# Last self-attention of a two-layer perceiver block: weighed V with columns in rows, exponentials divided before the weighing, the weighing one step later

## Chip, cores, metric

One core of one Trainium2 chip. The metric is the device time of one execution in microseconds (us), the median of several runs. Engines: PE or TensorE (matmuls, transpositions through an identity), VectorE (DVE), ScalarE (ACT), GpSimd (POOL), and SyncE (SP), which issues DMAs.

## The reference, cut to what matters

Six sublayers act on x of 128 batches x 32 tokens x 256 features: cross-attention, self-attention, a mixture of experts, cross-attention, self-attention (the one changed), and a linear layer with quantised weights and activations. The last two:

```python
qkv = einsum('bse,ef->bsf', layernorm(x), W_qkv)      # 256 -> 3 x 16 heads x 64
q, k = rotary(q), rotary(k)
scores = einsum('bqhd,bkhd->bhqk', q, k) / sqrt(64)    # 32 x 32 for each batch and head
weights = softmax(where(mask, scores, -1e9))           # causal mask
out = einsum('bhqk,bkhd->bqhd', weights, v)            # batch, 32, 16 x 64
x = x + einsum('bsf,fe->bse', out, W_out)              # 1024 -> 256
...
x = x + bit_linear(layernorm(x), weight)               # rounded to whole numbers, 256 -> 256
```

## The kernel before, in words

The kernel is written for the engines directly: each engine has a queue of its own in program order, and semaphores hold it where it needs another's result. Each sublayer is a stage. The last stage, `SelfAttention1`, does the last self-attention and the quantised linear layer (`BitLinear`).

The 4096 rows of x are 32 groups of 128 rows (4 batches of 32 tokens, `BPG` = 4). The stage is a loop of 42 steps g, written out by hand in `steps()`: in step g every engine does its share of group g (projections, rotation), of group g-1 (scores and softmax), of group g-2 (attention turned, projected out and added to X), of group g-3 (statistics for the last norm), and of the linear layer of group g-9 (`last`). Once in four steps come the jobs for four groups together: with g mod 4 = 1 the norm's statistics (`ln.take_stats`), with 2 its scaling, with 3 its transposition on PE (`ln.turn`, 8 transposes) and its split into a high and a low part on ScalarE and VectorE (`prepare`); and, from step 6 on, `quantise` with g mod 4 = 3 and `round_z` with g mod 4 = 0, on VectorE.

For float32 precision the projections are split products: every 128-row piece of weights and data is taken as high and low part in three matmuls, so one projection `project(g, i, c)` (i = 0, 1, 2 for Q, K, V, c the half of 512 columns) is 6 matmuls of 512 columns, and `project_out` is 24 of 256 columns. All these stand under line L223. Plain float32 matmuls (scores L865, weighing L914) are two instructions each in the trace.

PE's order in a step: project (0,0), (0,1); `turn_out(g-2, 0)` (4 transposes of the attention output, L1870); project (1,0), (1,1); `turn_out(g-2, 1)`; `turn` (0,0), (0,1) (rotated Q, L1857); scores(g-1) (64 products, 128 instructions); project (2,0); turn (1,0); `project_out(g-2)`; `ln.turn` in every fourth step; turn (1,1); project (2,1); `bit.turn` (2 transposes into bank z, L1750); weigh(g-1) (64 products, L914); `bit.product` (2 bfloat16 matmuls, L1767).

VectorE's order: rotate (0,0), (0,1); `attn_lo` 0; rotate (1,0), (1,1); `attn_lo` 1; softmax(g-1); the projected attention of g-2 added to X (L2031, which empties bank o); prepare; the norm's statistics or scaling; the last norm's statistics of g-3; quantise or round_z; the attention of g-1 divided by the sums out of PSUM (L2052); `bit.add` (L1774). ScalarE's: `attn_hi` 0, 1; `keep_turned` (0,0), (0,1); the exponentials of g-1 (L871); `keep_v` 0 (L1937); `keep_turned` (1,0); prepare; `keep_turned` (1,1); `keep_v` 1; `bit.keep_turned` (zT for the product, L1758). GpSimd adds the two halves of each rotation (L2067). The data all lie in SBUF here; the only DMAs are the loads of weights before the loop and eight stores of the result.

PSUM has 8 banks: two for the scores, two for the weighed V, and four in a `Ring` that hands them out in turn: a `take` gets the next of the four, and PE waits until the tile taken four takes before has been emptied by its reader (`s_v` for V, `r_swap` for Q and K, `r_qkT` for rotated tiles, `xT_lo` for the norm, `s_x1` for bank o, `bit_zT` for z, `bit_x` for the linear layer's product).

Of the kernel before, what the change touches and what calls it, by code (L numbers as in the profile page):

```python
# [16 lines left out]
P = 128  # L17
# [93 lines left out]
class Signals:  # L111


    def __init__(self, nc, stack):
# [14 lines left out]
        for tag, names in (("x0", "qkvo"), ("s0", "qkv"), ("moe", ("router",)), ("x1", "qo"),  # L129
# [31 lines left out]
        self.s_score, self.s_max, self.s_shift, self.s_exp, self.s_probT, self.s_inv, self.s_pv, self.s_out = (  # L161
            count("s_" + n, grid(SELF, g)) for n in ("score", "max", "shift", "exp", "probT", "inv", "pv", "out"))
        self.s_sum = count("s_sum", grid(("s1",), g))
# [23 lines left out]
        self.a_T, self.a_hi, self.a_lo = (count("a_" + n, grid(g, half)) for n in ("T", "hi", "lo"))  # L187
# [646 lines left out]
class HeadOrder:  # L834


    def __init__(self, R, head, cells):
        self.R, self.NH = R, H // R
        self.cells = cells
        self.column = {head(r, n): (r * self.NH + n) * T for r in range(R) for n in range(self.NH)}  # L840


class SelfSoftmax:


    def __init__(self, s, tag, order, tiles, score, scale, bound):
        self.s, self.tag, self.order, self.t, self.score, self.scale, self.bound = s, tag, order, tiles, score, scale, bound

    def cell(self, a):
        return a.rearrange("p (r n q) -> p r n q", r=self.order.R, q=T)  # L850

    def stat(self, a):
        return a.rearrange("p (r n) -> p r n", r=self.order.R)

    def scores(self, pe, g, q_k):
        s, tag, R = self.s, self.tag, self.order.R
        if g:
            if self.bound is None:
                pe.wait_ge(s.s_shift, tag, g - 1)
            else:  # L860
                pe.wait_ge(s.s_masked, g - 1)
        for heads, q, k in q_k(g):
            for b in range(BPG):
                for r in range(R):
                    ins = pe.do.matmul(self.score[b * T:(b + 1) * T, r, heads, :], q(b, r), k(b, r), start=True, stop=True)  # L865
        ins.then_inc(*s.s_score.at(tag, g))

    def exponent(self, act, g):
        s, tag, e = self.s, self.tag, g % 2
        act.wait_ge(s.s_shift, tag, g)  # L870
        act.do.activation(self.t["prob"][e][:, :], self.t["shifted"][e][:, :], ACT.Exp,  # L871
                          scale=self.scale if self.bound is None else 1.0).then_inc(*s.s_exp.at(tag, g))

    def softmax(self, dve, g):
        s, tag, t, e = self.s, self.tag, self.t, g % 2
        R, NH = self.order.R, self.order.NH
        src = self.score
        dve.wait_ge(s.s_score, tag, g)
        if g >= 2:
            dve.wait_ge(s.s_exp, tag, g - 2)  # L880
            dve.wait_ge(s.s_probT, tag, g - 2)
            dve.wait_ge(s.s_out, tag, g - 2)
        if self.bound is not None:
            for r in range(R):
                ins = dve.do.scalar_tensor_tensor(out=self.cell(t["shifted"][e][:, :])[:, r], in0=self.score[:, r], scalar=self.scale,
                                                  in1=self.bound.unsqueeze(1).to_broadcast([P, NH, T]), op0=ALU.mult, op1=ALU.min)
            ins.then_inc(*s.s_masked.at(g))
            dve.wait_ge(s.s_masked, g)
            src = self.cell(t["shifted"][e][:, :])
# [6 lines left out]
        if g >= 2:  # L896
            dve.wait_ge(s.s_pv, tag, g - 2)
# [5 lines left out]
        if len(own.shape) == 4:  # L903
            sums = sums.rearrange("p r (m e) -> p r m e", m=own.shape[2])
# [1329 lines left out]
```

## Time and profile before

| what | value |
|---|---|
| median of 3 runs | 2792.21 us (2787.71 to 2792.39) |
| profiled execution, time | 2789.23 us |
| profiled execution, span of its instructions | 2787.4 us |
| PE busy | 2515.0 us, 90% |
| VectorE busy | 1788.0 us, 64% |
| ScalarE busy | 1231.2 us, 44% |
| GpSimd busy | 796.2 us, 29% |
| mean granted PE clock | 0.958 of full speed |

The last stage's loop runs from about 2185 to the end. Busy times are of one profiled execution; an engine that is busy nearly all the time of a stage sets its length, unless it is held by waits shorter than a row shows. In rows of instructions in order of time, the first number is the start in us, the second the time to the end of the last instruction of the row; matmuls overlap, so the time that work costs is read from start to start. What stands in brackets is idle time of the engine before the row, and who ended it.

### The profile page before, as it was taken

What the parts mean: (1) busy time and instruction counts of PE and PEld (TensorE: products, weight loads), DVE (VectorE), ACT (ScalarE), POOL (GpSimd) and SP (SyncE); (2) the same over time, 40 slices, a digit from 0 to 9 for tenths busy, and PEclk for the clock granted to TensorE, in tenths of its full rate; (3) what the DMA queues carried; (4) which work ended last, traced back from release to release, by engine and by line L of the source; (5) the groups of instructions that cost most, each with busy time, mean ns of one, the idle gap of its engine ahead of it and who ended that gap; (6) DMA issues with size and microseconds to landing.
All of it is one profiled execution on the core that took longest, in us unless ns stands there. A gap on an engine that the chain in (4) does not pass through costs nothing. (4 is left out here: it accounts for less than half of the span.)

```text
span 2787.4 us, 101550 instructions
## 1 busy us (share of the span) xinstructions
PE 2515.0 (90%) x44320; PEld 1970.7 (71%) x44320; DVE 1788.0 (64%) x3820; ACT 1231.2 (44%) x2700; POOL 796.2 (29%) x696
## 2 busy tenths in 40 slices
PE   7999999999979866999996788889898799999997
PEld 6878788887845544666664677767776688888885
DVE  5666666666647754111112688888877778888886
ACT  5555555555534523222222566666664323333332
POOL 3222222222221211333333433333321232333321
PEclk9999999999989967999998899999999899999998
DMA  5333333333313113111112577676665100000000
GB/s 189 102 95 100 101 84 98 101 102 95 90 39 109 45 43 129 45 44 42 44 44 79 174 213 210 193 209 194 198 192 137 66 3 3 10 10 10 10 10 25
DMA packets 154328, 256.90 MB, mean 92 GB/s; under 512 B 24344, under 2 KB 102300, under 8 KB 144672
## 3 DMA queue, kind: packets, MB, share of 16 engines
q1 hardware_dynamic: 147072, 233.62, 28.6%
q0 software_dynamic: 6816, 16.79, 1.9%
q8 instruction: 352, 5.77, 0.9%
q14 instruction: 88, 0.72, 0.1%
HBM read 149.78 MB, written 57.80 MB: 74 GB/s over the span
## 5 line engine op out<-in xcount | busy, mean ns | idle before, releaser
L795 POOL TENSOR_TENSOR ctxT_x_lo<-ctx_in_x,ctxT_x_hi 128x514 fp32r<-128x514 f32 x256 | 306.4, 1198 | 890.6 <-ACT ctxT_x_hi L613 890.5
L671 DVE TENSOR_REDUCE neg_max_x<-ps_score_x 128x2 f32<-128x514 f32 x512 | 330.2, 686 | 303.3 <-PE ps_score_x L527 302.4
L635 ACT ACTIVATE prob_x<-ps_score_x,neg_max_x 128x257 f32<-128x257 f32 x1024 | 403.6, 480 | 227.5 <-DVE neg_max_x L671 227.5
L538 PE MATMUL ps_v_x<-v_wide_x,probT_x 128*32 128x68 f32 x18432 | 334.4, 225 | 71.8 <-DMA v_wide_x<-v_out_x 33.0
L538 PEld LDWEIGHTS ps_v_x<-v_wide_x,probT_x 128*32 128x32 f32 x18432 | 290.2, 109 | 147.1 <-issue 92.5
L695 DVE STREAM_TRANSPOSE probT_x<-prob_x 128x1152 f32<-128x1152 f32 x256 | 342.2, 1337 | 0.0
L2067 POOL TENSOR_TENSOR rot_s<-turned_s,swapped_s 128x512 f32<-128x512 f32 x128 | 163.5, 1291 | 300.1 <-DVE swapped_s L1996 255.1
L626 ACT ACTIVATE kT_x<-ps_x,bias_k 128x257 f32<-128x257 f32 x256 | 122.1, 477 | 234.8 <-PE ps_x L223 234.7
L1617 DVE TENSOR_TENSOR hid_moe<-ps_up_moe,silu_moe 128x512 f32<-128x512 f32 x71 | 49.1, 692 | 253.1 <-PE ps_up_moe L1429 253.1
L223 PE MATMUL ps_x<-ctxT_x_hi,w_v_x_hi 128*128 128x288 f32 x512 | 167.7, 328 | 25.5 <-DVE attn_x L715 13.7
L527 PE MATMUL ps_score_x<-kT_x,q_x 32*64 32x257 f32 x4096 | 178.0, 402 | 4.8 <-ACT prob_x L635 4.1
L223 PE MATMUL ps_x<-ctxT_x_hi,w_q_x_hi 128*128 128x288 f32 x512 | 168.0, 328 | 13.0 <-POOL ctxT_x_lo L795 12.7
L223 PE MATMUL ps_s<-w_qkv_s_hi,xT_s_hi 128*128 128x512 f32 x384 | 164.4, 428 | 1.6 <-DVE xT_s_lo L361 1.6
L613 ACT ACTIVATE ctxT_x_hi<-ctx_in_x 128x514 fp32r<-128x514 f32 x256 | 160.2, 627 | 0.0
L223 PE MATMUL ps_x<-ctxT_x_hi,w_k_x_hi 128*128 128x258 f32 x512 | 158.1, 309 | 0.0
L223 PE MATMUL ps_x<-ctxT_x_lo,w_q_x_hi 128*128 128x288 f32 x512 | 153.8, 300 | 0.0
L223 PE MATMUL ps_x<-ctxT_x_hi,w_q_x_lo 128*128 128x288 f32 x512 | 153.8, 300 | 0.0
L223 PEld LDWEIGHTS ps_x<-ctxT_x_hi,w_v_x_hi 128*128 128x128 f32 x512 | 96.2, 188 | 81.1 <-issue 48.7
L223 PE MATMUL ps_s<-w_qkv_s_lo,xT_s_hi 128*128 128x512 f32 x384 | 152.5, 397 | 0.2 <-issue 0.2
L223 PE MATMUL ps_s<-w_qkv_s_hi,xT_s_lo 128*128 128x512 f32 x384 | 152.5, 397 | 0.0
L223 PE MATMUL ps_x<-ctxT_x_lo,w_v_x_hi 128*128 128x288 f32 x512 | 151.6, 296 | 0.0
L223 PE MATMUL ps_x<-ctxT_x_hi,w_v_x_lo 128*128 128x288 f32 x512 | 150.9, 295 | 0.0
(241 smaller groups left out, 5697.3 us busy)
## 6 DMA issues: line engine op xcount, KB each, us to landing
ctx_in_x<-ctx SPq DMA_DIRECT2D x64, 1028.0 KB, 5.8
v_wide_x<-v_x SPq DMA_DIRECT2D x512, 76.5 KB, 2.1
v_out_x<-v_x SPq DMA_DIRECT2D x128, 306.0 KB, 3.7
v_wide_x<-v_out_x SPq DMA_DIRECT2D x512, 76.5 KB, 2.7
w_moe<-moe_experts SPq DMA_DIRECT2D x8, 1536.0 KB, 9.7
y_in_x<-y_out SPq DMA_DIRECT2D x16, 512.0 KB, 5.1
v_wide_s<-v_s SPq DMA_DIRECT2D x32, 136.0 KB, 2.5
X<-x SPq DMA_DIRECT2D x8, 512.0 KB, 12.5
```

Of the source, the lines that this page charges most:

```text
L223: last = pe.do.matmul(out, a, b, start=n == 0, stop=n == len(steps) - 1)
L527: ins = pe.do.matmul(self.ps[m * 2 * T:(m + 1) * 2 * T, r, 0:S], q, self.kT[b % 3][rows, m, 0:S], start=True, stop=True)
L538: ins = pe.do.matmul(self.ps_v[r * T:(r + 1) * T, b % 2, :, :], self.probT[b % 3][:, r, n * T:(n + 1) * T], self.v_wide[b % 4][:, :, r, n, ...
L613: act.do.activation(self.ctxT[b % 3].hi[:, :, 0:S], self.ctx_in[g % 2][:, :, j, :], ACT.Copy).then_inc(*s.ctx_hi.at(tag, b))
L626: act.do.activation(out, src, ACT.Identity, bias=self.biases["k"][:, m:m + 1]).then_inc(*s.k.at(tag, b, m))
L635: act.do.activation(self.prob[b % 3][:, r, 0:S], self.ps[:, r, 0:S], ACT.Exp, bias=self.neg_max[b % 2][:, r:r + 1]).then_inc(*s.exp.at(tag ...
L671: dve.do.tensor_reduce(self.neg_max[b % 2][:, r], self.ps[:, r, 0:S], AX_X, ALU.max, negate=True).then_inc(*s.neg_max.at(tag, b, half))
L695: dve.do.transpose(flat(self.probT[b % 3]), flat(self.prob[b % 3])).then_inc(*s.prob_T.at(tag, b))
L795: pool.do.tensor_tensor(self.ctxT[b % 3].lo[:, :, 0:S], self.ctx_in[g % 2][:, :, j, :], self.ctxT[b % 3].hi[:, :, 0:S].bitcast(F32), ALU.s ...
L1617: dve.do.tensor_tensor(self.hid[t % 2][:, :], self.up_ps[t % 2][:, :], self.silu[t % 2][:, :], ALU.mult).then_inc(*s.hid.at(t))
L2067: pool.do.tensor_tensor(self.rot[e][:, :, :], self.turned[e][:, :, :], self.swapped[e][:, :, :], ALU.add).then_inc(*s.r_rot.at(g, i, c))
```

## The change

- The weighing swaps its operands: V is the stationary one (32 rows x 64 columns) and the turned probabilities stream (32 columns). The result has the head's 64 columns in rows, two heads beside each other, which is the form `project_out` needs; so `turn_out` goes, with its two takes from the ring. ScalarE and VectorE split it into high and low part straight from the PSUM tile. Scores and weighed V now share four banks, one for each batch.
- The exponentials are divided by their sums in SBUF (128 x 512) before they are turned, and no longer the weighed V (128 x 1024) after it. `shifted` goes: masking, shift and exponentials work in place in `prob`.
- weigh(g-2) now stands in step g, between the first and second projection, not weigh(g-1) near the end of it.
- `bit.turn` moves ahead of project (2,1); `bit.product` comes right behind that projection. ScalarE's order stays.
- VectorE: both `attn_lo` come behind the first rotation; softmax is cut into `shift` and `normalise`, with all the statistics, scaling and quantising between them, and the addition to X and `prepare` behind `normalise`.

```diff
 class SelfSoftmax:
+    def __init__(self, s, tiles, ps, bound):
+        self.s, self.t, self.bound = s, tiles, bound
+        self.out = ps[:, :, 0:F1 // BPG].rearrange("p b (n q) -> p b n q", q=T)
+        self.score = ps[:, 0:2, F1 // BPG:2 * F1 // BPG].rearrange("p r (n k) -> p r n k", k=T)
...
+    def scores(self, pe, g, q, k):
         if g:
+            pe.wait_ge(s.s_masked, g - 1)
+            pe.wait_ge(s.a_lo, g - 1, 1)
...
+    def normalise(self, dve, g):
+        dve.wait_ge(s.s_exp, "s1", g)
+        dve.do.tensor_reduce(t["sums"][e][:, :], prob[:, :, :], AX_X, ALU.add).then_inc(*s.s_sum.at(g))
+        dve.wait_ge(s.s_sum, g)
+        dve.do.reciprocal(t["inv"][e][:, :], t["sums"][e][:, :]).then_inc(*s.s_inv.at("s1", g))
+        dve.wait_ge(s.s_inv, "s1", g)
+        dve.do.tensor_tensor(prob[:, :, :], prob[:, :, :], t["inv"][e][:, :].unsqueeze(2).to_broadcast([P, H, T]), ALU.mult).then_inc(
+            *s.s_norm.at(g))
...
+        dve.do.transpose(flat(t["probT"][e]), flat(prob)).then_inc(*s.s_probT.at("s1", g))
...
+    def weigh(self, pe, g, v):
+        s, probT = self.s, self.t["probT"][g % 2]
+        pe.wait_ge(s.s_probT, "s1", g)
+        if g:
+            pe.wait_ge(s.a_lo, g - 1, 1)
+        for n in range(H // 2):
+            for r in range(2):
+                for b in range(BPG):
+                    rows, head = slice(b * T, (b + 1) * T), 2 * n + r
+                    ins = pe.do.matmul(self.out[r * D1:(r + 1) * D1, b, n, :], v[rows, head * D1:(head + 1) * D1],
+                                       probT[rows, r * H // 2 + n, :], start=True, stop=True)
+        ins.then_inc(*s.s_pv.at("s1", g))
...
 SelfAttention1.tensor
             if now:
                 project(g, 0, 0)
+            if out:
+                weigh(g - 2)
+            if now:
                 project(g, 0, 1)
-            if out:
-                turn_out(g - 2, 0)
-            if now:
                 project(g, 1, 0)
                 project(g, 1, 1)
-            if out:
-                turn_out(g - 2, 1)
-            if now:
                 turn(g, 0, 0)
                 turn(g, 0, 1)
...
             if now:
                 turn(g, 1, 1)
-                project(g, 2, 1)
             if 0 <= last < G:
                 self.bit.turn(pe, last)
-            if before:
...
-                self.soft.weigh(pe, g - 1, self.out, self.v[(g - 1) % 2], D1)
+            if now:
+                project(g, 2, 1)
             if 0 <= last < G:
                 self.bit.product(pe, last)
 SelfAttention1.vector
             if now:
                 rotate(g, 0, 0)
-                rotate(g, 0, 1)
             if out:
                 attn_lo(g - 2, 0)
+                attn_lo(g - 2, 1)
             if now:
+                rotate(g, 0, 1)
                 rotate(g, 1, 0)
                 rotate(g, 1, 1)
-            if out:
-                attn_lo(g - 2, 1)
             if before:
-                self.soft.softmax(dve, g - 1)
+                self.soft.shift(dve, g - 1)
+            if 0 <= g - 3 < G:
+                self.bit.take_stats(dve, g - 3)
+            if n < SG and j == 1:
...
+            if n < SG and j == 2:
+                self.ln.scale(dve, n)
+            if 0 <= done < SG:
+                if jd == 1:
+                    self.bit.quantise(dve, done)
+                if jd == 2:
+                    self.bit.round_z(dve, done)
+            if before:
+                self.soft.normalise(dve, g - 1)
             if out:
                 dve.wait_ge(s.a_o_ps, g - 2)
                 dve.do.tensor_tensor(self.X[:, g - 2, :], self.X[:, g - 2, :], banks["o", g - 2][:, 0:D], ALU.add).then_inc(
                     *s.s_x1.at(g - 2))
             if n < SG and j == 3:
                 prepare(n)
...
```

## Rows read from the trace of the kernel before

**Rows 1.** Busy time (instructions) of PE, PEld, DVE, ACT, POOL, last stage

```profile
2200.00:2787.40 587.40, 564.13 (x10852) 487.66 (x10852) 472.49 (x1033) 171.95 (x326) 169.63 (x136) 0.98 0.03 10
```

**Rows 2.** PE in order of time, one step: start, length, engine, line, instructions

```profile
2641.13 0.60 PE L1870 MATMUL ps_s<-constants,attn_s 128*128 128x128 f32 x4
2641.49 0.48 PE L223 MATMUL ps_s<-w_qkv_s_hi,xT_s_hi 128*128 128x512 f32 x1
...
2644.36 0.60 PE L1870 MATMUL ps_s<-constants,attn_s 128*128 128x128 f32 x4
...
2645.77 1.29 PE L865 MATMUL ps_score_s<-kT_s,qT_s 64*32 64x32 f32 x128
2646.99 0.50 PE L223 MATMUL ps_s<-w_qkv_s_hi,xT_s_hi 128*128 128x512 f32 x1
...
2652.11 0.48 PE L223 MATMUL ps_s<-w_qkv_s_hi,xT_s_hi 128*128 128x512 f32 x1
...
2653.59 0.38 PE L1750 MATMUL ps_s<-constants,xn_bit 128*128 128x128 f32 x2
2653.90 1.99 PE L914 MATMUL ps_out_s<-v_s,probT_s 32*32 32x64 f32 x128
...
2655.97 0.48 PE L223 MATMUL ps_s<-w_qkv_s_hi,xT_s_hi 128*128 128x512 f32 x1
```

**Rows 3.** PE in order of time, in the first self-attention

```profile
841.72 0.86 PE L1040 MATMUL ps_score_s<-kT_s,q_s 32*64 32x32 f32 x64
842.51 3.70 PE L1001 MATMUL ps_s<-xT_s,w_k_s 128*128 128x512 f32 x8
```

**Rows 4.** Instruction groups, last stage, DVE: busy us, mean ns, then idle before

```profile
L885 DVE SCALAR_TENSOR_TENSOR shifted_s<-ps_score_s,constants 128x256 f32<-128x256 f32 x64 | 24.2, 420 | 19.8 <-PE ps_score_s L865 19.8
```

**Rows 5.** DVE in order of time, in a step with quantising

```profile
2450.07 0.69 DVE L892 TENSOR_TENSOR shifted_s<-shifted_s,neg_max_s 128x512 f32<-128x512 f32 x1
2451.46 0.71 DVE L898 STREAM_TRANSPOSE probT_s<-prob_s 128x512 f32<-128x512 f32 x1 [0.70 <-ACT prob_s L871]
2452.10 0.64 DVE L899 TENSOR_REDUCE sums_s<-prob_s 128x16 f32<-128x512 f32 x1
2452.78 0.25 DVE L905 RECIPROCAL inv_s<-sums_s 128x16 f32<-128x16 f32 x1
2453.41 0.42 DVE L2031 TENSOR_TENSOR X<-X,ps_s 128x256 f32<-128x256 f32 x1 [0.38 <-PE ps_s L223]
2454.54 1.29 DVE L361 TENSOR_TENSOR xT_s_lo<-ps_s,xT_s_hi 128x512 fp32r<-128x512 f32 x2 [0.71 <-ACT xT_s_hi L354]
2455.75 0.42 DVE L1700 BATCH_NORM_STATS2 stats_bit<-X 128x6 f32<-128x256 f32 x1
...
2456.30 1.37 DVE L1721 TENSOR_SCALAR xn_bit<-X,mv_bit,rstd_bit 128x256 f32<-128x256 f32 x4
...
2459.36 1.22 DVE L2052 TENSOR_TENSOR attn_s<-ps_out_s,inv_s 128x1024 f32<-128x1024 f32 x1
```

**Rows 6.** ACT in order of time, end of the step of rows 2

```profile
2653.79 0.60 ACT L1937 ACTIVATE v_s<-ps_s 128x512 f32<-128x512 f32 x1 [0.79 <-PE ps_s L223]
2654.28 0.38 ACT L1758 ACTIVATE zT_bit<-ps_s 128x256 bf16<-128x256 f32 x1
```

**Rows 7.** ACT and PE in order of time, after the last projection

```profile
2768.18 0.38 ACT L1758 ACTIVATE zT_bit<-ps_s 128x256 bf16<-128x256 f32 x1 [6.60 <-PE ps_s L1750]
...
2768.62 0.39 PE L1767 MATMUL ps_s<-wq_bit,zT_bit 128*128 128x256 bf16 x2 [0.48 <-ACT zT_bit L1758]
```

**Rows 8.** PE in order of time, two idle times near the end

```profile
2759.80 1.09 PE L1870 MATMUL ps_s<-constants,attn_s 128*128 128x128 f32 x8 [2.98 <-DVE attn_s L2052]
2762.62 0.55 PE L223 MATMUL ps_s<-w_out_s_hi,attnT_s_hi 128*128 128x256 f32 x1 [1.73 <-DVE attnT_s_lo L2005]
...
2767.76 0.38 PE L1750 MATMUL ps_s<-constants,xn_bit 128*128 128x128 f32 x2
```

**Rows 9.** PE busy time (instructions) and granted clock, one us there

```profile
2761.00:2762.00 1.00, 0.00 (x0) 0.50 1.03 418
```

More of the change, by code:

```diff
@@ L160, in __init__ @@
         self.s_v = count("s_v", grid(("s1",), g, half))
-        self.s_score, self.s_max, self.s_shift, self.s_exp, self.s_probT, self.s_inv, self.s_pv, self.s_out = (
-            count("s_" + n, grid(SELF, g)) for n in ("score", "max", "shift", "exp", "probT", "inv", "pv", "out"))
-        self.s_sum = count("s_sum", grid(("s1",), g))
+        self.s_score, self.s_max, self.s_shift, self.s_exp, self.s_probT, self.s_inv, self.s_pv = (
+            count("s_" + n, grid(SELF, g)) for n in ("score", "max", "shift", "exp", "probT", "inv", "pv"))
+        self.s_out = count("s_out", grid(("s0",), g))
+        self.s_sum, self.s_norm = (count("s_" + n, grid(g)) for n in ("sum", "norm"))
         self.m_xT, self.m_zero, self.xn_left = count("m_xT", grid(s, k)), count("m_zero", [()]), [
@@ L186, in __init__ @@
         self.s_masked = count("s_masked", grid(g))
-        self.a_T, self.a_hi, self.a_lo = (count("a_" + n, grid(g, half)) for n in ("T", "hi", "lo"))
+        self.a_hi, self.a_lo = (count("a_" + n, grid(g, half)) for n in ("hi", "lo"))
         self.a_o_ps, self.s_x1 = count("a_o_ps", grid(g)), count("s_x1", grid(g))
@@ L1818, in turn_before, with weighed, half @@
         return (n // 4, n // 2 % 2, n % 2) if n >= 0 else None
+    def weighed(self, c):
+        return self.soft.out[:, 2 * c:2 * c + 2, :, :]
+    def half(self, a, c):
+        return a[:, :].rearrange("p (n b q) -> p b n q", b=BPG, q=T)[:, 2 * c:2 * c + 2, :, :]
     def steps(self):
@@ L1858, in turn, with scores, weigh @@
             ins.then_inc(*s.r_T.at(g, i, c))
-        def q_k(g):
-            at = lambda a, n: (lambda b, r: a[g % 2][r * D1:(r + 1) * D1, n, b * T:(b + 1) * T])
-            return [(n, at(self.qT, n), at(self.kT, n)) for n in range(self.soft.order.NH)]
-        def turn_out(g, c):
-            bank, emptied = banks.take(("attn", g, c), s.a_lo, g, c)
-            pe.wait_ge(s.s_out, tag, g)
-            if emptied:
-                pe.wait_ge(*emptied)
-            for n in range(4):
-                ins = pe.do.transpose(bank[:, n * P:(n + 1) * P], self.attn[:, c * 512 + n * P:c * 512 + (n + 1) * P], ident[:, :])
-            ins.then_inc(*s.a_T.at(g, c))
+        def scores(g):
+            at = lambda a: (lambda b, n, r: a[g % 2][r * D1:(r + 1) * D1, n, b * T:(b + 1) * T])
+            pe.wait_ge(s.r_qkT, g, 1, self.NB - 1)
+            self.soft.scores(pe, g, at(self.qT), at(self.kT))
+        def weigh(g):
+            pe.wait_ge(s.s_v, tag, g, self.NB - 1)
+            self.soft.weigh(pe, g, self.v[g % 2])
         def project_out(g):
@@ L1900, in tensor @@
             if before:
-                pe.wait_ge(s.r_qkT, g - 1, 1, self.NB - 1)
-                self.soft.scores(pe, g - 1, q_k)
+                scores(g - 1)
             if now:
@@ L2003, in attn_lo @@
             dve.wait_ge(s.a_hi, g, c)
-            at = slice(c * 512, (c + 1) * 512)
-            dve.do.tensor_tensor(self.attnT.lo[:, at], banks["attn", g, c][:, :], self.attnT.hi[:, at].bitcast(F32),
+            dve.do.tensor_tensor(self.half(self.attnT.lo, c), self.weighed(c), self.half(self.attnT.hi, c).bitcast(F32),
                                  ALU.subtract).then_inc(*s.a_lo.at(g, c))
```

136 lines of the change are left out of this document (36 added, 100 removed).

## The prediction

> **What bounds the kernel now.** I read the page first (its chain that ended last is almost all tensor engine), then the busy time of the last stage, then one step of its tensor queue, then the other engines' queues in the same steps. The change touches the last stage alone. There the tensor engine is busy 564 of 587 us and VectorE 472 [rows 1]; so the tensor engine sets the step, with VectorE close behind. One step without the extra work of every fourth one runs from a transposition of attention at 2641.13 through the next step's first projection at 2655.97: 14.84 us, and two projections of 2.87 us (2641.49 to 2644.36) close the ring: 17.71 us [rows 2]. No row in it shows an idle time before it. The sum below is made against the profiled execution, 2789.23 us with a span of 2787.4; the median of the runs is 2792.21, so I add the sum to the median.
>
> **What the change takes from the tensor queue.** The eight transpositions of attention go. The first four take 0.36 (2641.13 to 2641.49) [rows 2]. A lone projection after a transposition takes 1.48 (2652.11 to 2653.59), while a pair takes 2.87, so the second takes 1.39 and a change of kind costs 0.09 [rows 2]. Each group of four costs some 0.44, together 0.88 us a step. That change of kind comes back, since the weighing now stands between two projections: +0.09. The transposition for the last linear layer now follows another one and not a projection, which saves such a change of kind: -0.1.
> The weighing itself has the same 128 instructions (64 products), but they stream 32 columns over weights of 64 columns, where they streamed 64 over 32. Before: from 2653.90 to the next projection at 2655.97 is 2.07, of which I give the product's two instructions 0.15: 1.92 [rows 2]. The new shape is not in this stage. Bounds: the scores of this stage, 128 instructions streaming 32 columns, take 1.22 (2645.77 to 2646.99) [rows 2]; the scores of the first self-attention have exactly the new tile, 32 rows by 64 columns, and take 0.79 for 64 instructions (841.72 to 842.51), 1.58 for 128 if nothing of it is start-up [rows 3]. I take 1.4, since part of those 0.79 is start-up, and keep 1.22 and 1.58. Gain 0.5 a step.
> The rule of the Trainium skill (TensorEngine Tiling (Array Packing), Instruction Overhead) that every matmul has some 60 cycles of overhead, so that 1 column takes as long as 60, speaks against this gain: by it the weighing would stay at 1.92. The trace disagrees: instructions of 32 columns start 9.5 ns apart where those of 64 start 15 ns apart [rows 2].
> So without waits a step is 0.88 + 0.5 + 0.1 - 0.09 = 1.4 us shorter: 16.3. Over 31 steps that would be 43 us.
>
> **A new wait in every step.** The bit layer's transposition now stands before the projection (2, 1), its product right after it; between them stood 1.9 us of weighing. ScalarE's order is not changed: it copies V of that projection first, then zT, for which the product waits. V's copy starts 0.20 after the projection's last issue (2653.79 against 2653.59), zT's copy 0.49 later [rows 2, 6]; a product starts 0.44 after the start of its zT copy [rows 7]. The tensor engine stands 1.14 us before each product. Behind it in the queue is the next step's projection. There are 23 steps with projections and a product (g = 9 to 31). Net there: -1.4 + 1.14 = -0.27, on a light step.
>
> **A new wait in every fourth step.** VectorE's order is changed: the addition of the projected attention to X, which empties a bank of the ring of four, and `prepare`, which empties two more and makes the next normalised input, stood before the quantising; now they stand behind quantising and `normalise`. In a step with g mod 4 = 3 the ring's takes are o, xT, xT, rot, z, qkv(2, 1), product: z gets the bank of o, the projection that of the first xT. Time from the step's first projection: 1.48 + 1.4 weighing + 1.48 + 2.8 for three projections + 1.41 - 0.44 for the rotated turns + 1.22 scores = 9.35 [rows 2]. VectorE begins the shift at 9.45: masking 0.79, maximum 0.7, addition 0.7, so 11.65 [rows 4, 5]. The statistics take 0.55 (2455.75 to 2456.30), the quantising 3.06 (2456.30 to 2459.36) [rows 5]: 15.25. Exponentials are long there. Normalise: sums 0.68 (2452.10 to 2452.78), reciprocal 0.3, multiplication 0.7 as the addition over the same 512 columns, transposition 0.64 (2451.46 to 2452.10), in all 2.35: 17.6 [rows 5]. The addition to X takes 0.4: 18.0. The tensor engine is through with its last rotated turn at 9.35 + 5.12 (2646.99 to 2652.11) + 0.8 for eight turns of the norm (two groups of 0.36 and a little) = 15.3 [rows 2]. It waits 2.8 us, turns z for 0.2, waits until the first half of `prepare` (0.68 of 1.29 [rows 5]) is done at 18.7, starts the projection at 18.8, ends at 20.25, waits 1.14, and the next step starts at 21.55. Before, such a step was 17.71 + 0.85 = 18.6. So +3.0 us. Five steps have all of this (11, 15, 19, 23, 27); in step 7 no z and no product exist, but the projection waits for the addition to X: 19.6 against 18.2, +1.4. In step 31 there is no `prepare`, the product waits for the addition instead: +0.5.
> VectorE's own work: the new multiplication, 0.7, replaces that over 1024 columns, 1.22 [rows 5]. It saves 0.5 us a step on an engine that isn't the bound and counts nothing by itself. In light steps the work in the place of the quantising is shorter, so the addition to X is done about when zT is: up to 0.3 more in a few steps, 1 us in all. The second rotation starts later, behind both `attn_lo`: 4.95, through GpSimd at about 7.6, when the tensor engine gets to it (7.55): nothing. ScalarE has idle time for the same two copies. No DMA moves. The last, emptied steps: scores now wait for `attn_lo` (+1), the weighed output no longer waits for its multiplication behind the rounding (-1): nothing, with 1 us either way.
>
> **Sum without the clock.** Steps 1 to 8: step 1 has no weighing (-1.9), five light ones -1.4 each (-7.0), step 3 about -1.0, step 7 +1.4: -8.5. Steps 9 to 31: seventeen light ones at -0.27 (-4.6), +1.0 for the addition, five heavy at +3.0 (+15.0), step 31 +0.5: +11.9. Together +3 us. Each 0.1 us of weighing is 3 us: 1.22 gives -2.5, 1.58 gives +8.5.
>
> **The clock.** A heavy step now has 2.8 + 0.5 + 1.14 = 4.4 us of idle tensor engine within 6.2 us. In the trace there is one like stretch near the end: 2.98 idle, eight transpositions, 1.73 idle [rows 8]. The granted clock was 0.50 (1.2 GHz) by 2761, before the second idle time was over [rows 9]. So I expect it to fall in most of the six heavy steps. The 24 matmuls after it, the whole projection of the output, took from 2762.62 to 2767.76, 5.14 us [rows 8]; at full clock half of that would do, so up to 2.6 us are lost. In the heavy step the projection at 18.8 alone would lose 1.4, which is the lower bound of a fall that comes in time for it. I take 2.3 a fall, near the row, and five falls in six steps: +11. Total +14: 2787.4 to 2801.4 in span, 2806 in the median.
>
> **Rivals.**
> (a) Both waits, the clock falls in most heavy steps: 2806 (2799 to 2814). For it: the queue orders and the rows above. Chance 0.42.
> (b) Both waits, the clock holds, because z's transpositions and the projection break the idle stretch: +3, 2795 (2789 to 2799). Chance 0.22.
> (c) The other side: the weighing is faster than the scores, as the four row groups and two column halves overlap fully. At 1.0 us (a little under 8 ns apart, against the 9.5 of the scores) and a full clock the sum is 3 - 12 = -9: 2783. It decides from 1.15 us down. Against it: the wider weights. Chance 0.09.
> (d) The waits don't bind, since I misread an order: the 43 us come in full, 2749; with the wait before the product alone, about 2773. Against it: the ScalarE order is plain in the code. Chance 0.07.
> (e) The skill's rule holds for the small weighing in effect, 1.9 us: +16 on (a) or (b), 2811 to 2822. Against it: the scores' 1.22. Chance 0.12.
> (f) A fall costs 5 us or more, as the idle before the product keeps the clock low into the next step, or light steps lose it too: 2825 to 2840. Chance 0.08.
> A measurement of this kernel can't tell 0.2%, 5.6 us, from no change. Faster: (c), (d), nearly all: 0.16. Same: (b) mostly: 0.20. Slower: (a), (e), (f) and the rest: 0.64. The range from 2784 to 2830 leaves out (d), some of (c) and of (f); that of the likeliest alone is 2799 to 2814.
>
> **What would show it.** In the profile after: the product idle before, some 1.1 us on the zT copy, 23 times; z or the projection (2, 1) waiting some 2.8 us for the addition to X (VectorE) and 0.5 for xT_lo every fourth step; step lengths of some 17.4, 17.7 and 21.5 (15.9 before g = 9); 0.50 clock in windows at steps 11, 15, ...; the weighing's start-to-next at 1.4. I am wrong if the product starts without an idle time, if heavy steps stay under 19, or if the weighing isn't between 1.2 and 1.6.

## Result and profile after

The changed kernel takes 2822.52 us (median of 4 runs, 2808.95 to 2829.36) against 2790.15 for the one before (4 runs, 2787.71 to 2792.39). The ratio is 1.0105, its 95% interval 1.0073 to 1.0136: slower by some 32 us. That lies in the stated range of 2784 to 2830 and in the predicted direction, 16 us above the predicted 2806, and outside the 2799 to 2814 that rival (a) had for itself. The profiled execution takes 2821.87 us with a span of 2819.7, so it stands for the median. The page of the kernel after begins like this:

```profile
span 2819.7 us, 100964 instructions
PE 2500.6 (89%) x44064; PEld 1940.0 (69%) x44064; DVE 1772.9 (63%) x3820; ACT 1233.1 (44%) x2700; POOL 797.4 (28%) x696
```

Stages ahead of the changed one move from trace to trace (the loop begins anywhere from 2202.90 in experiment 9 to 2219.88 in experiment 5), so I compare the loop alone: from the start of the scores in step 2 to the start of those in step 31, 29 steps. Before, that is 2213.19 to 2736.76, 523.6 us; after, 2210.23 to 2767.67, 557.4 us. The loop has the whole difference, +33.9. What follows it takes 50.6 before and 52.0 after.

The waits of the tensor queue in the loop (engine and tile that waited, line, what released it; total us, times, longest) are these after, and of the kernel before the one row that counts:

```profile
PE ps_s L1758 <- ACT zT_bit L1749: 16.4, 17, 1.0
PE ps_s L854 <- issue: 11.0, 6, 2.1
PE ps_s L1741 <- DVE X L2023: 10.8, 5, 2.6
PE ps_s L1758 <- DVE X L2023: 5.7, 5, 1.2
PE ps_s L904 <- issue: 2.9, 4, 0.9
PE ps_s L224 <- DVE X L2023: 2.0, 1, 2.0
```

```profile
PE ps_score_s L865 <- issue: 3.8, 3, 1.6
```

The reader is to see two kinds. The named waits are the predicted ones: the product (L1758) on ScalarE's copy of zT or, some 0.1 us later, on the addition to X, and the norm's transpositions (L1741) on the addition to X. The rows with "issue" name no releaser: the tensor engine stands still in the middle of the scores (L854) or the weighing (L904), and no engine is late. With three small ones at L224 (1.5) and one at L1850 (0.6) they make 16.0 us in 14 times. The prediction has no such term, though the kernel before shows it too.

**A light step.** The tensor queue of one after (start, duration, engine, line, operation, shapes, count; in brackets the idle time before it and who ended it), which answers to [rows 2]:

```profile
2471.77 1.29 PE L854 MATMUL ps_s<-kT_s,qT_s 64*32 64x32 f32 x128
...
2481.28 0.39 PE L1758 MATMUL ps_s<-wq_bit,zT_bit 128*128 128x256 bf16 x2 [0.96 <-ACT zT_bit L1749]
2481.43 0.48 PE L224 MATMUL ps_s<-w_qkv_s_hi,xT_s_hi 128*128 128x512 f32 x1
2483.01 1.49 PE L904 MATMUL ps_s<-probT_s,v_s 32*64 32x32 f32 x128
2484.42 0.50 PE L224 MATMUL ps_s<-w_qkv_s_hi,xT_s_hi 128*128 128x512 f32 x1
...
2489.79 1.29 PE L854 MATMUL ps_s<-kT_s,qT_s 64*32 64x32 f32 x128
```

The weighing takes 1.41 us (2483.01 to 2484.42) where I had 1.4 and, before, 1.92. The rule of the Trainium skill (TensorEngine Tiling (Array Packing), Instruction Overhead), by which I had put it at 1.92 in rival (e), doesn't show here: its instructions start 11 ns apart, those of before 15. The first projection ahead of it takes 1.58 (2481.43 to 2483.01) where a lone one took 1.48 [rows 2]. The product waits 0.96 for zT, and ScalarE's two rows show why: V's copy comes first, as it did before [rows 6].

```profile
2480.36 0.60 ACT L1918 ACTIVATE v_s<-ps_s 128x512 f32<-128x512 f32 x1 [1.02 <-PE ps_s L224]
2480.85 0.38 ACT L1749 ACTIVATE zT_bit<-ps_s 128x256 bf16<-128x256 f32 x1
```

Light steps from step 9 on without a gap or a fall take 17.67 us where the product waits for zT and up to 17.95 where it waits for the addition to X (step 24). The one shown, step 16, takes 18.02, since its projection of the output starts 0.33 later behind the turns than in other steps; the earlier ones without a product take 16.08 to 16.13, where 15.9 was predicted.

**A heavy step.** The tensor queue and VectorE's of one in which the clock held, the latter answering to [rows 5]:

```profile
2368.00 1.29 PE L854 MATMUL ps_s<-kT_s,qT_s 64*32 64x32 f32 x128
...
2377.93 0.44 PE L1741 MATMUL ps_s<-constants,xn_bit 128*128 128x128 f32 x2 [2.45 <-DVE X L2023]
2381.15 0.39 PE L1758 MATMUL ps_s<-wq_bit,zT_bit 128*128 128x256 bf16 x2 [0.96 <-ACT zT_bit L1749]
```

```profile
2371.46 0.42 DVE L1691 BATCH_NORM_STATS2 stats_bit<-X 128x6 f32<-128x256 f32 x1
2372.01 1.35 DVE L1712 TENSOR_SCALAR xn_bit<-X,mv_bit,rstd_bit 128x256 f32<-128x256 f32 x4
...
2375.06 0.68 DVE L883 TENSOR_REDUCE sums_s<-prob_s 128x16 f32<-128x512 f32 x1
2376.06 0.69 DVE L887 TENSOR_TENSOR prob_s<-prob_s,inv_s 128x512 f32<-128x512 f32 x1
2376.86 0.71 DVE L893 STREAM_TRANSPOSE probT_s<-prob_s 128x512 f32<-128x512 f32 x1
2377.49 0.38 DVE L2023 TENSOR_TENSOR X<-X,ps_s 128x256 f32<-128x256 f32 x1
```

Everything from the statistics to the turned probabilities stands ahead of the addition to X (2377.49); the transposition of z starts 0.44 after it. This step takes 22.48 us with an idle time of 0.57 in its weighing; the other one in which the clock held, step 19, has none and takes 21.66. 21.55 was predicted.

**The clock.** In three of the six heavy steps it fell on the named waits, in two it held, and in one it fell behind an idle time without a releaser (below). These windows of one of them (length, busy time of the tensor engine, granted clock, share and GB/s of the DMAs) show it at 1.00 in the last scores, an idle microsecond, 0.69 where z's transpositions and the projection behind them run, 0.50 (1.2 GHz) where the product waits (busy 0.55) and still in the next step's weighing, and 0.90 in the microsecond after:

```profile
2613.00:2614.00 1.00, 1.00 (x11) 1.00 0.00 0
...
2616.00:2617.00 1.00, 0.00 (x0) 1.00 0.00 0
2619.00:2620.00 1.00, 1.00 (x5) 0.69 0.00 0
2620.00:2621.00 1.00, 0.55 (x2) 0.50 0.00 0
2625.00:2626.00 1.00, 1.00 (x93) 0.50 0.00 0
2626.00:2627.00 1.00, 1.00 (x50) 0.90 0.08 16
```

The step took 23.98 us, 2.3 more than the 21.66 in which the clock held: the price that the prediction took. The other two are not alike: step 27 was at 0.50 for half as long again and took 27.17, of which 2.1 are a gap and 3.4 the fall; step 7 was at 0.50 for half as long and lost some 1.3 (21.21 with a gap of 0.2, against 19.94 in experiment 9, which pays 0.27 for its split and shows no fall there). And four falls stand behind idle times without a releaser, as this one in the scores of step 15 (103 instructions, 1.78 us of nothing, the remaining 25):

```profile
2448.13 1.07 PE L854 MATMUL ps_s<-kT_s,qT_s 64*32 64x32 f32 x103
2450.98 0.33 PE L854 MATMUL ps_s<-kT_s,qT_s 64*32 64x32 f32 x25 [1.78 <-issue]
```

In the three light steps (4, 12 and 21) the fall adds 1.6 to 1.8 us to the gap itself. In step 15, a heavy one, it adds 0.2 (23.64 against 21.66 and the gap of 1.78): the wait before z is 0.99 there and not 2.45, so the lost time was time that the engine would have waited.

**Where the gaps stand.** The profile names nobody for an idle time with "issue", but the traces say more than that. I count every instruction of the tensor queue: weight loads, products, and the queue's own. In the loops of the kernel before, the one after and experiments 1 to 5 and 7 to 9 there are 137 such idle times, and in each trace all lie at multiples of 256 instructions from each other, give or take one. So the place belongs to the queue and not to the moment: in step 15 the scores stop behind 103 instructions in the kernel after and in experiments 1, 2, 3, 4, 5 and 8. This is experiment 5:

```profile
2442.90 1.07 PE L854 MATMUL ps_s<-kT_s,qT_s 64*32 64x32 f32 x103
2445.76 0.33 PE L854 MATMUL ps_s<-kT_s,qT_s 64*32 64x32 f32 x25 [1.78 <-issue]
```

And all 137 end 2.2 to 3.3 us after a transfer of 16 KB of instructions started on DMA queue 8. For the gap in step 15 of the kernel after, which ends at 2450.98, it is the one transfer between 2448 and 2449 (start about 2448.6, no other until the gap ends):

```profile
q8 instruction: 1, 0.02, 5.9%
```

So what runs short is, as far as these traces can show it, the tensor queue's next block of instructions. Not every multiple of 256 has a gap (63 in the loop after have none), and the experiments say what makes one late.

### The profile page after: what moved, and what is told of

Its sections match the earlier page's. It is cut to its first block and busy times, and to the rows that moved or that the text cites. A ratio compares the mean times of both kernels' runs of the same rounds, so it can differ in the third digit from the quotient of the medians.

```text
span 2819.7 us, 100964 instructions
## 1 busy us (share of the span) xinstructions
PE 2500.6 (89%) x44064; PEld 1940.0 (69%) x44064; DVE 1772.9 (63%) x3820; ACT 1233.1 (44%) x2700; POOL 797.4 (28%) x696
## 5 line engine op out<-in xcount | busy, mean ns | idle before, releaser
L224 PE MATMUL ps_x<-ctxT_x_hi,w_v_x_hi 128*128 128x288 f32 x512 | 167.5, 327 | 25.6 <-DVE attn_x L716 13.8
L224 PE MATMUL ps_x<-ctxT_x_hi,w_q_x_hi 128*128 128x288 f32 x512 | 167.3, 327 | 12.1 <-POOL ctxT_x_lo L796 11.1
L224 PE MATMUL ps_s<-w_qkv_s_hi,xT_s_hi 128*128 128x512 f32 x384 | 168.4, 439 | 4.2 <-DVE xT_s_lo L362 2.3
L224 PE MATMUL ps_x<-ctxT_x_hi,w_k_x_hi 128*128 128x258 f32 x512 | 158.1, 309 | 0.0
L224 PE MATMUL ps_s<-w_qkv_s_lo,xT_s_hi 128*128 128x512 f32 x384 | 156.9, 409 | 1.1 <-issue 1.1
L224 PE MATMUL ps_s<-w_qkv_s_hi,xT_s_lo 128*128 128x512 f32 x384 | 157.1, 409 | 0.0
L224 PE MATMUL ps_x<-ctxT_x_lo,w_q_x_hi 128*128 128x288 f32 x512 | 153.1, 299 | 0.0
L224 PE MATMUL ps_x<-ctxT_x_hi,w_q_x_lo 128*128 128x288 f32 x512 | 153.0, 299 | 0.0
L224 PEld LDWEIGHTS ps_x<-ctxT_x_hi,w_v_x_hi 128*128 128x128 f32 x512 | 96.1, 188 | 81.1 <-issue 48.7
L224 PE MATMUL ps_x<-ctxT_x_lo,w_v_x_hi 128*128 128x288 f32 x512 | 151.6, 296 | 0.0
L224 PE MATMUL ps_x<-ctxT_x_hi,w_v_x_lo 128*128 128x288 f32 x512 | 151.0, 295 | 0.0
```

Of the source, the lines that this page charges most:

```text
L224: last = pe.do.matmul(out, a, b, start=n == 0, stop=n == len(steps) - 1)
```

## Experiments

Below, "the loop" is always those 29 steps in the profiled execution; the ratio is that of the medians to the kernel before, with its 95% interval.

**1. zT ahead of V on ScalarE.** The rest is the changed kernel.

```diff
             if now:
                 keep_turned(g, 1, 1)
-                keep_v(g, 1)
             if 0 <= last < G:
                 self.bit.keep_turned(act, last)
+            if now:
+                keep_v(g, 1)
```

> The changed kernel, but ScalarE copies zT before the copy of V's second half (its order follows the tensor queue). Theory 1 (my steps): the idle time before the product on the zT copy (0.96 us a step, 23 times) goes, but in the steps with rounding or norm statistics the product's bank is then awaited, emptied by the addition to X at about the same moment, so those gain 0.1 us or less; the steps with scaling gain some 0.8, the steps with quantising some 1.1. In all -11 us against the changed kernel: about 2811. Rival 2 (the zT copy is the whole of the loss in light steps): 23 x 1.0 = -23 us, about 2799. Rival 3 (most of the loss is in gaps without a releaser and the clock, whatever the waits): within 3 us of the changed kernel.

Measured: 2808.46 us, 1.0053 (1.0034 to 1.0071), near the first theory's 2811; loop 538.3, 19 less than after. The wait on zT is gone, and behind it the addition to X shows:

```profile
PE ps_s L1741 <- DVE X L2024: 9.9, 5, 2.5
...
PE ps_s L1758 <- DVE X L2024: 9.2, 13, 1.2
```

So one swap of two copies on ScalarE, an engine that is 44% busy over the kernel and 29% in this stage, is worth 14 us. The heavy steps' wait stays, as it should.

**2. Quantising behind `prepare` on VectorE.** The rest is the changed kernel.

```diff
-            if 0 <= done < SG:
-                if jd == 1:
-                    self.bit.quantise(dve, done)
-                if jd == 2:
-                    self.bit.round_z(dve, done)
+            if 0 <= done < SG and jd == 2:
+                self.bit.round_z(dve, done)
...
             if n < SG and j == 3:
                 prepare(n)
+            if 0 <= done < SG and jd == 1:
+                self.bit.quantise(dve, done)
```

> The changed kernel, but VectorE quantises behind normalise, the addition to X and the split of the next normalised input. Theory 1: the 2.4 us before z in every fourth step goes, an idle time of about 1 us before the projection (2,1) on the split's low part appears; 6 steps x 1.5 us plus some clock falls of 2 us each saved: -9 to -15 us against the changed kernel, about 2810. Rival 3 (clock falls and gaps come by themselves, the heavy step's excess is not this order): within 3 us. Rival 4 (VectorE is the bound in the heavy step): what the tensor engine gains there is given back in the next step by a late rotation, below 5 us gained.

Measured: 2808.96 us, 1.0060 (1.0040 to 1.0080), where 2810 was expected; loop 536.8, 21 less than after. The intervals of this kernel and the one after just touch (1.0080 and 1.0073); the medians lie 14 us apart. L1741's wait on the addition to X is gone from the heavy steps, zT's stays:

```profile
PE ps_s L1758 <- ACT zT_bit L1749: 14.5, 15, 1.0
```

The granted clock is part of it. I add up, over windows of the loop, the time at 1.2 GHz (a window's length times twice what its granted clock lacks to 1.00): none before, 34.1 us after, 6.8 here, both parts of it behind gaps (1.70 and 2.06 us). No heavy step fell on its waits.

**3. Both edits together.**

> The changed kernel with both small repairs: ScalarE copies zT first, and quantising stands behind the split. Theory 1: the two are not additive in light steps, since the product's bank is still emptied by the addition to X behind the rounding or the norm statistics (1.06 us in steps with rounding, 0.23 in those with statistics, none in those with scaling). Against the changed kernel: the repair of ScalarE gave 14 us, that of quantising 14; together -22 to -28, about 2795. Rival: they are the same loss twice, and together give 16 us at most, 2805.

Measured: 2795.43 us, 1.0012 (0.9993 to 1.0030); loop 531.0. The two causes add up to the change's loss: without them it is no slower. But the loop is still 7.4 longer than before, though its weighing is shorter and its transpositions are gone. The waits say where: 14.9 us in 8 idle times without a releaser within the scores (with those elsewhere 21.2, against 4.0 before), and 7.5 before the product on the addition to X; and 20.5 us at 1.2 GHz, where the kernel before has none.

**4. The new form of the weighing, the order of before.** On the tensor engine weigh(g-1) stands at the end of the step again, behind project(2,1) and `bit.turn`; on VectorE `normalise`, the addition to X and `prepare` come right behind `shift`, ahead of statistics, scaling and quantising.

```diff
                 project(g, 0, 0)
-            if out:
-                weigh(g - 2)
-            if now:
                 project(g, 0, 1)
...
                 turn(g, 1, 1)
+                project(g, 2, 1)
             if 0 <= last < G:
                 self.bit.turn(pe, last)
-            if now:
-                project(g, 2, 1)
+            if before:
+                weigh(g - 1)
             if 0 <= last < G:
                 self.bit.product(pe, last)
```

> The new form of the weighing (columns in rows, no transposition of attention, division before turning) in the queue orders of the kernel before: weighing of the group one step back, between the last transposition and the product; on VectorE shift, normalise, addition to X, split, statistics, quantising in that order. Theory 1: the form alone saves 1.4 us in each of 31 steps, no new wait: light steps 16.3 to 16.5 us, 43 us less than before, about 2747 to 2755. Rival 4 (VectorE, 14.8 us of work a step and 16.4 in the quantising one, becomes the bound): light steps 16.8 and more, 2760 to 2775. Rival 5 (the form itself is the loss: dense bursts of small instructions starve the tensor queue): gaps without a releaser stay as in the changed kernel, some 16 us in all, and the time is 2765 or more.

Measured: 2785.29 us, 0.9974 (0.9955 to 0.9992); loop 520.5. I missed by 30 us. The two rivals on record don't explain it: the same work of VectorE fits in steps of 16.55 in experiment 5, where they are 17.25 here, and the idle times without a releaser are 8.0 us, not some 16. The trace names a wait that I had left out:

```profile
PE ps_s L1850 <- POOL rot_s L2036: 20.9, 29, 1.0
PE ps_s L854 <- issue: 6.1, 4, 2.0
```

In one step, the tensor engine, VectorE and GpSimd:

```profile
2489.79 0.66 PE L1850 MATMUL ps_s<-constants,rot_s 128*128 128x128 f32 x4 [0.68 <-POOL rot_s L2036]
```

```profile
2485.78 1.28 DVE L1982 TENSOR_TENSOR attnT_s_lo<-ps_s,attnT_s_hi 128x512 fp32r<-128x512 f32 x2
2486.98 0.68 DVE L1972 TENSOR_TENSOR turned_s<-ps_s,constants 128x512 f32<-128x512 f32 x1
```

```profile
2488.46 2.54 POOL L2036 TENSOR_TENSOR rot_s<-turned_s,swapped_s 128x512 f32<-128x512 f32 x2 [1.16 <-DVE turned_s L1972]
```

Both `attn_lo` stand ahead of the second rotation, so GpSimd's addition is late by 0.7 us in every step. In the changed kernel the 1.4 us of weighing between the first two projections put the tensor engine that much later, and covered it. The place of the weighing, which looked like a part of the change that costs, earns about 0.7 a step.

**5. The changed kernel's tensor queue, the other two queues put right.** Edit 1 on ScalarE, and VectorE's order of experiment 4 (the same lines go from their place behind the quantising):

```diff
             if before:
                 self.soft.shift(dve, g - 1)
+                self.soft.normalise(dve, g - 1)
+            if out:
+                dve.wait_ge(s.a_o_ps, g - 2)
+                dve.do.tensor_tensor(self.X[:, g - 2, :], self.X[:, g - 2, :], banks["o", g - 2][:, 0:D], ALU.add).then_inc(
+                    *s.s_x1.at(g - 2))
+            if n < SG and j == 3:
+                prepare(n)
             if 0 <= g - 3 < G:
                 self.bit.take_stats(dve, g - 3)
```

> The changed kernel's tensor queue (weighing one step later, between the first two projections; product right behind the last projection), but ScalarE copies zT first and VectorE has the order of before. Theory 1: no new wait is left but the last projection's on the low part; 2750 to 2760, within 5 us of the kernel with the form alone. Rival 5' (gaps without a releaser come from the weighing standing only 4.9 us before the scores, two bursts of 256 instructions): this kernel keeps some 15 us of such gaps while the one with the weighing 7 us ahead has about 4, and lies 10 us above it. Rival 4 (VectorE the bound): 2765 to 2780.

Measured: 2769.56 us, 0.9909 (0.9879 to 0.9939); loop 503.6, 20 less than before, 17 less than in experiment 4. A light step takes 16.55 and a heavy one 18.41, with 0.39 of waiting on xT_lo. It comes out 10 above the upper end of the expectation. That is in the range of the rival that makes VectorE the bound, but the named waits left are 3.3 us in the whole loop (2.0 on xT_lo, 1.3 on GpSimd), so they aren't it. Of the waits left most have no releaser (some 11 us in the loop; 3.0 of L224's 5.2 lie behind its end). The rival that gave this queue more such gaps than that of experiment 4 and a longer time has the gaps right (11 against 8.0) and the time wrong:

```profile
PE ps_s L854 <- issue: 8.1, 5, 2.1
PE ps_s L224 <- issue: 5.2, 4, 3.0
```

**6. The same with the scores in two halves.** The gaps fall behind some 100 of the 128 short instructions. If they come from too many short instructions in a row, which use up a block of 256 in little time, a projection among them ends them.

```diff
                 project(g, 1, 0)
+            if before:
+                scores(g - 1, 0)
+            if now:
                 project(g, 1, 1)
...
-                scores(g - 1)
+                scores(g - 1, 1)
...
-        for n in range(H // 2):
+        for n in range(part * H // 4, (part + 1) * H // 4):
```

> The kernel with the orders put back (e5, 2770), but the scores in two halves of 128 instructions, the first between the projections (1,0) and (1,1). Theory B (gaps without a releaser inside the scores come from dense bursts of small instructions, used up faster than they are brought in): the gaps within the scores (8.1 us in five steps) mostly go, below 3 us in all; the split costs 0.15 to 0.3 us a step (two more changes of tile shape), 5 to 9 us, and so the time stays within 5 us of 2770. Rival C (the gaps come at fixed places of the instruction stream whatever stands there): the same number of gaps at the same steps, now elsewhere in the step, and 5 to 9 us slower.

Measured: 2757.06 us, 0.9888 (0.9860 to 0.9916): the best of all, 33 us below the kernel before and 65 below the changed one. The expectation was to stay within 5 us of 2770; the median is 12.5 below experiment 5's, though the two intervals overlap (0.9860 to 0.9916, 0.9879 to 0.9939). Each half takes 0.76 where one half of 1.29 would be 0.65, and a light step 16.82, 0.27 more than in experiment 5. That costs 8 us in the loop, and still it is 9.4 shorter (494.2). No idle time without a releaser is left in the loop, and the clock never falls there (3.4 us at 1.2 GHz in experiment 5); the first rows of the waits are now

```profile
PE ps_s L1742 <- DVE xn_bit L1734: 5.3, 1, 5.3
...
PE ps_s L224 <- issue: 3.0, 1, 3.0
```

The 3.0 without a releaser at L224 and the 5.3 at L1742 lie in the emptying steps behind the 29.

**7. Experiment 5 with a longer row of short instructions.** Every product of the weighing is done twice, with the same result.

```diff
-        for n in range(H // 2):
+        for n in [*range(H // 2)] * 2:
             for r in range(2):
```

> The kernel with the orders put back (e5), every product of the weighing done twice (256 instructions in a burst where there were 128, 512 with the weight loads). Theory B: the weighing costs 1.25 to 1.4 us more a step, 32 steps, 40 to 45 us, and on top gaps without a releaser inside the weighing and the scores grow from 11 us to 25 or more: 2835 and more. Rival C (gaps go by place, or by time): +40 to 45 us and gaps about as before, 2812 to 2818. It also gives the price of 128 such instructions without the change of shape.

Measured: 2933.61 us (one run), far above the 2835 "and more"; loop 656.0, 152 more than in experiment 5. Of these 41 are the doubled work (29 times 1.41), 60 idle time without a releaser (70.5 against 11), and the rest, some 50, is mostly the clock's.

```profile
PE ps_s L904 <- issue: 53.8, 28, 2.7
PE ps_s L854 <- issue: 13.7, 11, 2.2
```

```profile
2404.62 2.37 PE L904 MATMUL ps_s<-probT_s,v_s 32*64 32x32 f32 x218
2409.18 0.85 PE L904 MATMUL ps_s<-probT_s,v_s 32*64 32x32 f32 x38 [2.19 <-issue]
```

L904 had no gap in experiment 5 and has 28 here; time at 1.2 GHz goes from 3.4 to 133.1 us. All 42 gaps of the loop stand at multiples of 256 instructions: the place is the queue's, and the length of a row of short instructions decides how often the next block is late. The clock falls behind them.

**8. Experiment 5 without the swap on ScalarE**, so VectorE's order alone is put right.

> The changed kernel with VectorE's order of before alone (shift, normalise, addition to X, split, then statistics and quantising); ScalarE's order stays as the change left it. Theory 1: the waits on the addition to X go, the wait of 0.96 us (1.13 in step length) on the zT copy stays in 23 steps: the kernel with both orders back plus 26 us, 2796, between it and the changed kernel. Rival 2': once VectorE's order is back the rest hardly matters, within 10 us of 2770.

Measured: 2790.30 us, 1.0000 (0.9981 to 1.0019), 6 below the expected 2796; loop 527.5, 24.0 more than experiment 5: zT's wait in 22 steps of the loop. The row that is back:

```profile
PE ps_s L1758 <- ACT zT_bit L1749: 21.2, 22, 1.0
```

With `normalise`, the addition to X and `prepare` back in their places on VectorE (both `attn_lo` stay behind the first rotation) the changed kernel is as fast as the one before, and the swap of two copies is then worth 21 us, against 14 in the changed kernel, where the addition to X stands behind it.

**9. The changed kernel with the scores in two halves**, nothing else: the edit of experiment 6 on it.

> The changed kernel, all its orders kept, with the scores in two halves, the first between the projections (1,0) and (1,1). Theory B (dense bursts starve the tensor queue; gaps and the clock falls behind them are the part of the loss that my steps lack): the 16 us of gaps without a releaser go nearly all, with four clock falls of 1.7 us, and the split costs 0.27 us a step, 8 us: 13 to 16 us below the changed kernel, 2806 to 2810, while the waits before z and before the product stay as they were. Rival: the gaps move to the weighing (the waits before it let the queue run dry): below 8 us gained.

Measured: 2813.34 us, 1.0096 (1.0069 to 1.0123), less gained than the 13 to 16 expected; loop 547.4, 10.1 less than after. The gaps are gone but for 0.5 us, the named waits stay:

```profile
PE ps_s L1742 <- DVE X L2027: 12.3, 5, 2.5
PE ps_s L1759 <- ACT zT_bit L1750: 11.6, 12, 1.0
PE ps_s L1759 <- DVE X L2027: 11.5, 10, 1.2
```

In all five heavy steps that have z and a product the clock fell; they take 24.15 to 24.30. Without a gap ahead of it, one of them shows 0.71 right behind the first wait (2.47 us, to 2448.6) and 0.50 behind the second (0.96, to 2452.0):

```profile
2450.00:2451.00 1.00, 1.00 (x4) 0.71 0.00 0
2454.00:2455.00 1.00, 1.00 (x3) 0.50 0.00 0
```

So the falls in heavy steps need no gap, and the time at 1.2 GHz is 34.1 us as in the changed kernel: the falls behind gaps went, and more heavy steps fell on their waits. That is why the gain stayed small. By the medians the gain over the changed kernel isn't settled (the intervals 1.0069 to 1.0123 and 1.0073 to 1.0136 overlap); the loop's 10.1 is one execution of each.

**10. The kernel before with the scores in two halves.**

> The kernel before with the scores in two halves in the same place. Theory B: its three or four gaps (4 us) go, the split costs 0.27 us in 31 steps, 8 us: 3 to 5 us slower than before, 2795. If it is faster by 5 us or more, gaps that the profile of before doesn't show were costing it time in the runs that were not profiled.

Measured: 2792.02 us, 1.0004 (0.9988 to 1.0019), where 3 to 5 us more than before were expected; loop 527.8, 4.3 more than before. A light step takes 18.08 and had 17.71. The kernel before has 3.8 us of gaps in its scores; they are gone, and the split costs more than they did. It pays only where the gaps do.

## Why the prediction was right, and what it missed

The loop's +33.9 us taken apart. I add up the lengths of steps without a gap or a fall: 519.6 before, some 487 in the form of experiment 5 with its few waits taken off, and some 528 after. From the first to the second it is less work, from the second to the third the named waits (their idle times alone add up to 35.6; a light step is 1.13 longer for 0.96 of idle time). These two and the clock are estimates, good to a few us:

| term | predicted | measured in the 29 steps |
|---|---|---|
| less work, each step | -1.4 | about -1.2, in all some -33 |
| wait before the product | +1.14 | +1.13 on zT, 22 waits of 0.96 to 1.25 idle |
| heavy step, at full clock | 21.55 long | 21.66 long |
| all named waits | | some +41 |
| idle without a releaser | not in it | +12.0 (16.0 after, 4.0 before) |
| clock | +11, five falls of 2.3 | some +12: 7 in the heavy steps, 5 behind gaps |
| not placed | | some +2 |

- **The new wait in every step** came in its place, on zT and with its size; experiments 1 and 8 took it away and brought it back at 14 and 21 us. Rival (d), that the waits don't bind, is wrong.
- **The wait in every fourth step** came in its place too: the addition to X, 2.45 us where 2.8 was worked out, 0.16 on xT_lo where 0.5 was, and the step's length right within 0.11. Experiment 2 removes it.
- **The new form of the weighing** takes 1.41 (1.4 predicted; rival (c) asked for under 1.15, rival (e) for 1.9). Light steps were predicted as some 17.4 and took 17.67. The term "1.4 us shorter" was mis-sized by 0.2: half of it is the projection ahead of the weighing, 1.58 where I had 1.48: the change of kind, charged once, seems to be paid on both sides. Over 29 steps that is 6 us.
- **The clock.** The size of a fall was right for one of the three on the waits (2.3) and for experiment 9's five (2.2 to 2.4); the other two cost 1.3 and 3.4. The count wasn't right: three of six heavy steps on the waits, and four behind idle times that I hadn't foreseen. The total, 12 against 11, is right partly by chance. Rivals (b), no fall, and (f), falls of 5 us, are both wrong. The measured time lies at the edge of (e)'s 2811 to 2822, whose mechanism, a weighing of 1.9 us, is wrong too: a time alone doesn't pick the rival.
- **Not in the sum: idle times without a releaser.** The prediction says of the step it used that no row shows an idle time before it, which is true of that step and not of the loop: the waits of before had 3.8 us in 3 idle times of the scores. After, all of them make 16.0 us, 12 more than before, and the falls behind them some 5. With the 6 us of the step's work, and 4 less than forecast for the falls in heavy steps, that is 19 us; the profiled span is 18 above the predicted 2801.4. Their places, at multiples of 256 instructions behind a transfer of instructions, tie them to the queue's own supply, and experiments 6, 7, 9 and 10 to the length of a row of short instructions. This is the term that the sum put at nothing. The stated range was wide enough for it, and in that the number was lucky.
- **The second rotation** was put at nothing, "when the tensor engine gets to it". That holds only with the weighing between the projections; experiment 4 lost 0.7 us a step on it. The sentence that names the cover was right, and I forgot it myself when I moved the weighing.

Open: that the gaps wait for instructions is inferred from their places and the transfers; why one block comes late and another, with as many short instructions ahead of it, in time is not shown. Why L904 has short gaps (0.2 to 1.1 us) in the kernels where the product waits and none in experiments 4 and 5 isn't known, nor why the clock held in two heavy steps of the changed kernel and in none of experiment 9's.

## What to carry to other kernels

A form that saves work on the bound engine (here some 33 us in the loop) can lose more in the queues of engines that are half idle: after a reordering, ask for each product on the bound engine what stands ahead of its input in the other engine's queue, and put right the order there before judging the form. The same change with two queues put right and the scores halved is 1.1% faster than the kernel before, where as it stood it was 1.1% slower. Read the waits without a releaser over the whole loop and not in one clean step, count the instructions between them, and when a piece of work is moved, list first what it covered where it was.

## What the runs showed of the hardware

- The tensor engine stands still now and then with no releaser in the trace, by itself for 0.2 to 2.7 us, mostly late in a row of short instructions (32 columns, each with its own weights): 11.0 us in 6 times in the scores of the kernel after, behind 95 to 122 of 128, and 53.8 in 28 in the weighing with its row doubled to 256; none in the loop of experiment 6, where each row of 128 scores is cut into two of 64.
- All 137 such idle times in the loops of ten traces lie at multiples of 256 instructions of the tensor queue from each other, within one, and end 2.2 to 3.3 us after the start of a 16 KB transfer of instructions on DMA queue 8.
- The granted clock fell to 0.50 behind four of the six gaps of 1.7 to 2.1 us in the scores of the changed kernel (those of 1.70, 1.80, 1.78 and 1.83), at 1.6 to 1.8 us each in light steps and 0.2 in the heavy one; behind those of 1.82 and 2.09 it held. In heavy steps with 2.4 to 2.6 and 0.96 us of waiting it fell in two of four of the changed kernel, at 2.3 and 3.4, and in five of five of experiment 9, at 2.2 to 2.4.
- Products with 32 rows by 64 columns of weights and 32 streaming columns start 11 ns apart; those of the scores, 64 rows by 32 columns, 9.5; those of the old weighing, 32 by 32 with 64 streaming columns, 15.
